# Norm, projections and rotation of the sequence three ahead moved into the tail of a step, and the stored base formed by GpSimd

## What is computed

```
x + attention16(xn) + ffn(xn)
attention16: 16 heads of 8, rotated q and k, distance decay, causal softmax, Wo
ffn: n1 = layernorm(xn); rw = gating(n1)          (8 experts, softmax weights)
     q, k, v = sum over e of rw[e] * (n1 @ proj[e]);  soft = softmax(q k^T) v
     hs = xn + sum over e of rw[e] * (soft @ o_proj[e])
     rw2 = gating(layernorm(hs));  hs + sum over e of rw2[e] * gelu(n2 @ w1[e]) @ w2[e]
```

## Time and profile before

| what | value |
|---|---|
| median of 3 runs | 1389.92 us (1386.5 to 1391.0) |
| the profiled execution | 1386.97 us |
| its span, first to last instruction | 1385.1 us |
| TensorE busy | 1229.1 us, 89% |
| VectorE, ScalarE, GpSimd busy | 73%, 51%, 15% |
| chain that ended last, by engine | PE 68%, DVE 16%, issue 9%, SyncE's queue 4%, DMA 2%, ACT 1% |
| mean granted TensorE clock | 0.966 of 2.4 GHz |

### The profile page before, as it was taken

How to read it: one execution, slowest core, us unless ns; L and a number is a source line. 1 busy time by engine, 2 the same in 40 slices (tenths; PEclk the granted TensorE clock), 3 DMA queues, 4 the chain that set the end, 5 groups by cost and what they waited for, 6 DMA issues and landing times.

```text
span 1385.1 us, 33706 instructions
## 1 busy us (share of the span) xinstructions
PE 1229.1 (89%) x10780; PEld 938.4 (68%) x10780; DVE 1004.5 (73%) x3691; ACT 707.4 (51%) x1281; POOL 211.0 (15%) x325
## 2 busy tenths in 40 slices
PE   1249999999999999999999999999999979999998
PEld 0127777777777677777777777777777766777776
DVE  5547777777777777777777777777777657777653
ACT  1115555555555555555555555555555665555532
POOL 1011111121111222221111111112111200000000
PEclk9659999999999999999999999999999999999999
DMA  5312232222222222222322222222222106544344
GB/s 131 87 63 79 79 90 81 82 82 77 78 78 82 81 80 78 77 77 81 96 97 77 77 79 88 81 82 81 80 80 78 53 26 230 194 154 154 154 169 153
DMA packets 107942, 133.19 MB, mean 96 GB/s; under 512 B 18116, under 2 KB 87252, under 8 KB 99692
## 3 DMA queue, kind: packets, MB, share of 16 engines
q1 hardware_dynamic: 105668, 131.66, 29.6%
q10 hardware_dynamic: 2216, 0.80, 0.2%
HBM read 109.12 MB, written 21.54 MB: 94 GB/s over the span
## 4 chain that ended last, share of the span: by engine, by line
PE 68%; DVE 16%; issue 9%; SPq 4%; DMA 2%; ACT 1%; DVEq 0%; ACTq 0%
PE ps L1448 9%; PE ps L1493 9%; PE ps L1694 8%; PE ps L1449 8%; PE ps L1680 8%; PE ps L1321 4%; PE ps L1458 3%; PE ps L1425 2%; DVE mx L1070 2%; PE ps L1408 2%; SPq L415 2%; PE ps L1371 1%; PE ps L1507 1%; PE ps L1381 1%; DVE xn L894 1%
## 5 line engine op out<-in xcount | busy, mean ns | idle before, releaser
L1070 DVE TENSOR_REDUCE mx<-ps 128x4 f32<-128x1024 f32 (+1 forms) x192 | 234.9, 1223 | 89.4 <-PE ps L1381 80.0
L663 ACT ACTIVATE pr<-ps 128x1024 f32<-128x1024 f32 x192 | 195.8, 1020 | 138.4 <-PE ps L1408 93.7
L558 POOL TENSOR_TENSOR n1s<-rep,n1T 128x256 f32<-128x256 f32 x256 | 176.8, 728 | 254.3 <-DVE mpart L1084 254.3
L669 ACT ACTIVATE ps<-trn 128x1024 f32<-128x1024 bf16 x191 | 197.2, 1032 | 5.1
L1694 PEld LDWEIGHTS ps<-w2s,ats 128*128 128x128 f32 x1024 | 131.7, 192 | 49.8 <-issue 46.8
L1448 PE MATMUL ps<-n1s,wqk 128*128 128x256 f32 x512 | 163.0, 400 | 0.0
L1449 PE MATMUL ps<-n1s,wqk 128*128 128x256 f32 x512 | 152.7, 380 | 0.0
L1458 PE MATMUL ps<-wv,n1s 128*128 128x128 f32 x1024 | 141.6, 281 | 0.0
L1493 PE MATMUL ps<-wop,ats 128*128 128x128 f32 x1024 | 140.0, 294 | 0.0
L842 ACT ACTIVATE n1s<-ps 128x512 f32<-128x512 f32 x128 | 76.5, 597 | 122.6 <-PE ps L1680 121.5
L1694 PE MATMUL ps<-w2s,ats 128*128 128x128 f32 x1024 | 135.7, 276 | 0.5 <-DVE ats L1253 0.5
(11 more groups left out here) (228 smaller groups left out, 2038.3 us busy)
## 6 DMA issues: line engine op xcount, KB each, us to landing
rep<-scr_rw SPq DMA_DIRECT2D x32, 1024.0 KB, 5.0
stk<-scr_rw SPq DMA_DIRECT2D x16, 1024.0 KB, 8.1
stk<-scr_parts SPq DMA_DIRECT2D x896, 16.0 KB
scr_parts<-parts SPq DMA_DIRECT2D x64, 192.0 KB, 2.3
rots<-scr_rw SPq DMA_DIRECT2D x8, 1024.0 KB, 4.8
wqk<-scr_rw SPq DMA_DIRECT2D x8, 1024.0 KB, 8.9
stk<-scr_parts SPq DMA_DIRECT2D x128, 48.0 KB
xt<-in_x SPq DMA_DIRECT2D x32, 128.0 KB, 2.5
```

Source lines behind the costliest of these rows:

```text
L558: pool.tensor_tensor(n1s[:, e], rep[:, par, e], n1T[:, par], ALU.mult).then_inc(n1s_done, 1)
L663: act.activation(pr[:, Q, :, i], ps[:, S2[0]:S2[0] + NF], ACT.Exp).then_inc(exp_done, 1)
L669: act.activation(ps[:, S2[0]:S2[0] + NF], seeds[:, kind:kind + 1].broadcast_to((P, NF, 512)), ACT.Copy).then_inc(seed_done, 1)
L1070: dve.tensor_reduce(mx[:, min(i, 1)].rearrange("p (f h) -> p f h", f=NF)[:, :, h:h + n], ps[:, S1[0]:S1[0] + NF].rearrange("p f (h t) -> p ...
```

## The change

Norm transposes and both projections of sequence n+3 move into the tail of step n, instead of those of n+2 at its start; so does the rotation, between `add_x` and `add_hs`. They use the banks of `S1` and `PVB` there, and the transposed weights and maxima move to `G1`. ScalarE's `evac_norm` is split: `xnT` in the tail, `n1T` and the square at the start of the next step. All six row maxima now lie beside the gating's links, and `soft_max`, `normalise` and `soft_norm` at other links. GpSimd forms base, behind its `scale`. The diff, cut to its core (eight columns of indentation removed):

```diff
-GATE_MAX_AT = (7, 12, 17, 22)
+GATE_MAX_AT = (2, 7, 11, 16, 20, 24)
...
+FIRST, LATER = (G0, G1, G1), (S1[0], S1[1], PVB)
...
+    def add_base(n, u):
+        pool.wait_ge(hs_done, n + 1)
+        pool.wait_ge(xa_done, n + 1)
+        pool.wait_ge(base_stored, 16 * n)
+        hv = hs[:, T * n:T * n + T] if isinstance(n, int) else hs[:, bass.ds(n * T, T)]
+        pool.tensor_tensor(bs[:, u], hv, xa[:, u], ALU.add).then_inc(base_done, 1)
...
         if n_x:
             scale(n + 1, 1 - u)
+        add_base(n, u)
...
-    def evac_norm(b, par):
+    def evac_norm_x(b, banks):
         act.wait_ge(xzT_out, b + 1)
+        act.activation(xnT[:], ps[:, banks[0], 0:S], ACT.Copy).then_inc(xnT_done, 1)
+    def evac_norm_1(b, par, banks):
+        act.wait_ge(xzT_out, b + 1)
         if not isinstance(b, int) or b > 1:
             act.wait_ge(n1s_done, E * (b - 1))
-        act.activation(xnT[:], ps[:, G0, 0:S], ACT.Copy).then_inc(xnT_done, 1)
-        act.activation(n1T[:, par], ps[:, G0, S:2 * S], ACT.Identity, bias=lnp[:, 1:2],
+        act.activation(n1T[:, par], ps[:, banks[0], S:2 * S], ACT.Identity, bias=lnp[:, 1:2],
...
+        if not isinstance(b, int) or b > 1:
+            act.wait_ge(mT_out, b)
         act.wait_ge(rw_stored, 16 * b)
-        act.activation(rwT[0:E * T, 0:P], ps[0:E * T, S1[1], 0:P], ACT.Copy).then_inc(rwT_done, 1)
+        act.activation(rwT[0:E * T, 0:P], ps[0:E * T, G1, 0:P], ACT.Copy).then_inc(rwT_done, 1)
...
-        act.activation(mT[:], ps[0:3 * H, S1[0], 0:S // 2].bitcast(BF16), ACT.Copy).then_inc(mT_done, 1)
+        act.activation(mT[:], ps[0:3 * H, G1, P:P + S // 2].bitcast(BF16), ACT.Copy).then_inc(mT_done, 1)
...
-            evac_norm(n + 2, u)
+            evac_norm_1(n + 2, u, LATER)
         exps(n, 0)
...
         evac_pv(n, 1)
         if n_x >= 2:
+            evac_v(n + 2, u)
+        if n_x == 3:
+            evac_norm_x(n + 3, LATER)
+        if n_x >= 2:
             evac_weights(n + 2)
-            evac_v(n + 2, u)
         if n_x:
             evac_max(n + 1)
...
+    evac_norm_x(2, LATER)
...
-    def rotate(b, beside=None):
-        c = Chain(dve, rot_chain, b, ROT_LINKS, beside)
+    def rotate(b, banks):
+        c = Chain(dve, rot_chain, b, ROT_LINKS)
+        half = "p (a t) -> p a t"
         dve.wait_ge(rot_q_out, b + 1)
-        c.link(dve.tensor_tensor(rott[:, 0], ps[:, G1].rearrange("p (a t) -> p a t", a=2), cs[:, 0], ALU.mult))
+        c.add(dve.tensor_tensor(rott[:, 0], ps[:, banks[1]].rearrange(half, a=2), cs[:, 0], ALU.mult))
+        c.wait()
         c.add(dve.tensor_tensor(rot[:, 0], rott[:, 0, 0], rott[:, 0, 1], ALU.add))
         dve.wait_ge(rot_k_out, b + 1)
-        c.link(dve.tensor_tensor(rott[:, 1], ps[:, G1].rearrange("p (a t) -> p a t", a=2), cs[:, 1], ALU.mult))
+        c.add(dve.tensor_tensor(rott[:, 1], ps[:, banks[2]].rearrange(half, a=2), cs[:, 1], ALU.mult))
+        c.wait()
         c.link(dve.tensor_tensor(rot[:, 1], rott[:, 1, 0], rott[:, 1, 1], ALU.add))
...
         ins.then_inc(hs_done, 1)
-        dve.wait_ge(hs_done, n + 1)
-        dve.wait_ge(xa_done, n + 1)
-        dve.wait_ge(base_stored, 16 * n)
-        dve.tensor_tensor(bs[:, u], hv, xa[:, u], ALU.add).then_inc(base_done, 1)
...
         def beside_gating(k):
             next(norm, None)
             if k in GATE_MAX_AT:
-                next_max(2 + GATE_MAX_AT.index(k))
-            if k == 11:
+                next_max(GATE_MAX_AT.index(k))
+            if k == 17:
+                soft_max(n)
+            if k == 18:
                 normalise(n, 0)
-            if k == 14:
-                soft_max(n)
-            if k == 20:
+            if k == 28:
                 soft_norm(n)
         if n_x >= 2:
-            rotate(n + 2, beside_rotation)
-            next_max(1)
             gating(n + 2, T, 0, gate1, LG1, NORM1, 1, beside_gating)
             run(norm)
...
         add_x(n, u)
+        if n_x == 3:
+            rotate(n + 3, LATER)
         add_hs(n, u)
...
     max_parts(0)
+    rotate(2, LATER)
...
-    def norm_T(b, free):
+    def norm_T(b, banks, free):
...
-                ins = pe.transpose(ps[:, G0, (T * k + i) * P:(T * k + i + 1) * P], src[:, i], ident[:])
+                ins = pe.transpose(ps[:, banks[0], (T * k + i) * P:(T * k + i + 1) * P], src[:, i], ident[:])
...
-    def proj(b, side, prev):
+    def proj(b, side, banks, prev):
...
-            ins = mm(ps[:, G1, k * S:(k + 1) * S], wa[:, 2 * side + k], xnT[:], start=True, stop=True)
+            ins = mm(ps[:, banks[1 + side], k * S:(k + 1) * S], wa[:, 2 * side + k], xnT[:], start=True, stop=True)
         ins.then_inc((rot_q_out, rot_k_out)[side], 1)
...
-    def weights_T(b, old):
+    def weights_T(b, free):
         pe.wait_ge(rw_out, 3 * (b + 1))
-        if old:
-            pe.wait_ge(s1_read, UNITS * b)
-        else:
-            pe.wait_ge(rwT_done, b)
-        pe.transpose(ps[0:E * T, S1[1], 0:P], gt[:, 6, 0:T].rearrange("p i e -> p (i e)"), ident[:]
+        free()
+        pe.transpose(ps[0:E * T, G1, 0:P], gt[:, 6, 0:T].rearrange("p i e -> p (i e)"), ident[:]
                      ).then_inc(rwT_out, 1)
...
-        if k == 0:
-            pe.wait_ge(rwT_done, b + 1 if not isinstance(b, int) or b else 2)
-            pe.wait_ge(mT_done, b)
+        if k == 0 and front is not None:
+            pe.wait_ge(n1T_done, front + 1)
+            pe.wait_ge(rot_chain, ROT_LINKS * front + 1)
...
-        pv = ps[:, S1[0], 0:S // 2].bitcast(BF16)
+        pv = ps[:, G1, P:P + S // 2].bitcast(BF16)
...
+            if front is not None:
+                pe.wait_ge(rot_chain, ROT_LINKS * front + 3)
...
-    def soft_scores(n, free):
+    def soft_scores(n):
         pe.wait_ge(qkT_done, 2 * (n + 1))
-        free()
+        pe.wait_ge(hs_done, n)
...
-                unit1(n + 1, 1 - u, k)
-        if n_x >= 2:
-            norm_T(f, lambda: pe.wait_ge(ats_done, len(ATS_CHUNKS) * n))
+                unit1(n + 1, 1 - u, k, f if n_x >= 2 else None)
         unit2(n, u, 0)
         qk(n, 0)
-        if n_x >= 2:
-            proj(f, 0, lambda: pe.wait_ge(hs_done, n))
         qk(n, 1)
...
         if n_x >= 2:
-            proj(f, 1, lambda: pe.wait_ge(rot_chain, ROT_LINKS * f + 1))
             logits(f)
...
         qk(n, 6)
+        next_max(2)
         qk(n, 7)
-        pv(n, u, 0)
+        pv(n, u, 0, f if n_x >= 2 else None)
         if n_x == 0:
             logits2(0)
-        next_max(2)
+        next_max(3)
         unit2(n, u, 3)
-        soft_scores(n, (lambda: pe.wait_ge(rot_chain, ROT_LINKS * f + 3)) if n_x >= 2 else
-                    (lambda: pe.wait_ge(hs_done, n)))
+        soft_scores(n)
         ve(n, 0)
         out_T(n, 0)
         ve(n, 1)
         ve(n, 2)
-        next_max(3)
+        next_max(4)
         unit2(n, u, 4)
...
-        next_max(4)
+        next_max(5)
         unit2(n, u, 5)
         ve(n, 7)
         if n_x == 0:
             norm_T2(3)
         soft_T(n)
-        next_max(5)
         pv(n, u, 1)
         soft_av(n, (lambda: pe.wait_ge(lg_read, f + 1)) if n_x >= 2 else (lambda: None))
         out_T(n, 1)
         if n_x >= 2:
-            weights_T(f, True)
             proj_v(f, True)
+        if n_x == 3:
+            norm_T(g, LATER, lambda: pe.wait_ge(s1_read, UNITS * f))
+            proj(g, 0, LATER, lambda: None)
+        if n_x >= 2:
+            weights_T(f, lambda: None)
         if n_x:
             max_T(n + 1)
         att_T(n)
+        if n_x >= 2:
+            pe.wait_ge(rwT_done, f + 1)
+        if n_x:
+            pe.wait_ge(mT_done, n + 2)
         oe(n, 0)
         oe(n, 1)
         att_out(n)
+        oe(n, 2)
+        oe(n, 3)
+        if n_x == 3:
+            proj(g, 1, LATER, lambda: pe.wait_ge(xa_done, n + 1))
...
-        for e in range(2, E):
+        for e in range(4, E):
             oe(n, e)
...
     for k in range(UNITS):
         unit1(0, 0, k)
+    norm_T(2, LATER, lambda: pe.wait_ge(s1_read, UNITS))
+    proj(2, 0, LATER, lambda: None)
+    pe.wait_ge(rwT_done, 2)
     max_T(0)
+    proj(2, 1, LATER, lambda: None)
     step(0, 0, 3)
```

More of the change, by code:

```diff
@@ L813, in _ @@
             for b in range(2):
-                evac_norm(b, b)
+                evac_norm_x(b, FIRST)
+                evac_norm_1(b, b, FIRST)
                 evac_logits(b)
@@ L1181, in next_max @@
                         row_max(n + 1, k)
-                def beside_rotation(k):
-                    if k == 1:
-                        next_max(0)
                 norm = (layer_norm(n + 3, 1 - u) if n_x == 3 else layer_norm2(0) if n_x == 1 else
@@ L1206, in step @@
                 else:
-                    for k in range(1, ROT_LINKS + 1):
-                        beside_rotation(k)
-                    next_max(1)
                     if n_x == 0:
@@ L1227, in _ @@
                 norm = layer_norm(b + 1, 1 - b)
-                rotate(b)
+                rotate(b, FIRST)
```

(35 more changed lines are left out.)

## The result

The changed kernel took 1491.78 us (median of 4, 1483.31 to 1492.58) against 1389.76 us: ratio 1.0724, 95% interval 1.0681 to 1.0767. The forecast was 1456 with a range of 1412 to 1475: slower, by the forecast mechanism, but the loss is 102 us where 67 were worked out.

A forecast was written before the change was run, and what follows sets the result against it. TensorE, busy for 89% of the span, was taken to bound the kernel. 28 x (1.75 + 1.2) = 82.6, -14.4 old clock falls, -0.9: +67.3 on 1386.97, 1454.3; half of 2.95 added, 1456, range 1412 to 1475.

The forecast's parts named there:

- the forecast mechanism: Late base delays the `xt` load, gating and `unit1` number 1; TensorE idles 2.9 us and its clock falls; chance 0.60.
- The waits that go: TensorE's tail, `pv` to next step: the waits for weights and `att` go, 1.3 + 0.3 us.
- The load of `xt`: SyncE queue behind base: base at 3.15, `xt` issued at 4.6, landed at 7.1; the old 6.7 us to spare is gone.
- Landing at 7.1: `xt` lands 7.1 us into the step, 2.5 after its issue at 4.6, while gating starts at 4.7.
- The rest of the step: From `unit1` number 1: 8.9 us to `unit2`(4), 4.5 to `pv`(1), 11.3 to the next step.
- The price of the wait: `unit1` number 1 waits from 6.3 to 9.25, 2.9 us idle; the step is 1.75 longer than the steady 32.2.
- the sum without a clock fall: Whole step: 9.25 + 8.9 + 4.5 + 11.3 = 33.95 us.
- rounding the landing down to 7.0: First maximum put at 8.05 to 9.25, its start from 7.0 + 1.05 although the landing was 7.1.
- The clock: TensorE's clock falls behind the 2.9 us idle in nearly each step: 1.2 us taken, bounds nothing and 1.6.
- The rows at 5.13 us: Old kernel's last step: 5.13 us wait ahead of `att_T`, behind which eight `oe` products took 1.92 at the lower clock.
- that the clock would hold: Rival: TensorE stalls once per step but its clock does not fall, +33.7, 1421 to 1424 us; chance 0.20.
- that the load would be in time: Rival: `xt` lands before about 5.3, so `bn_stats` does not wait; by 4.8, 1359 us; chance 0.12.

The follow-up runs named there:

- e1: Changed kernel with SyncE's load of `xt` for the sequence three ahead moved ahead of the wait for base: 1369.97 us, ratio 0.9877.
- e3: Changed kernel with six extra never-read products on TensorE in the wait ahead of `unit1` number 1: 1445.0 us, ratio 1.0405.
- e9: Changed kernel with `add_hs` put back ahead of the rotation in VectorE's tail: 1405.58 us, ratio 1.0105.
- e10: Changed kernel with three extra never-read products on TensorE in the wait ahead of `unit1` number 1: 1461.21 us, ratio 1.052.
- e2: Changed kernel with base formed by VectorE again, right behind `add_hs`, the rotation staying ahead: 1442.96 us, ratio 1.0357.
- e4: Changed kernel with the load of `xt` issued later, behind the weights' spread copy and the store of the parts: 1630.25 us, ratio 1.1741.

## Why the prediction was right, and where it failed

- *The waits that go* (weights, `att`): right, neither is in the list any more.
- *The load of `xt`*: right, and the heart of it. Base at 3.15 was worked out, measured 3.45 (610.32 + 0.72): GpSimd's addition takes 0.72 (0.7 taken), its start 0.28 behind `add_hs` (0.1 taken). Landing at 7.1 was worked out, 7.33 measured in the step shown (607.59 to 614.92) and about 7.55 in the mean.
- *The rest of the step*: `unit2`(4) to `pv` 4.5, measured 4.49 (627.94 to 632.43); tail 11.3, measured 11.25 (632.43 to 643.68); `unit1`(1) to `unit2`(4) 8.9, about 9.1 at the full clock.
- *The price of the wait, first step that failed*: the sum without a clock fall, 33.95, is too small. Measured are 29.24 + 5.49 = 34.7 in the mean; only the quickest steps reach 34. `unit1` number 1 starts some 9.9 into the step and not at 9.25, so it waits 3.3 us and not 2.9: base is 0.3 later, from issue to reading the load takes 2.7 in the mean, where the median landing of 2.5 was put in, and rounding the landing down to 7.0 was wrong by itself. 28 x 0.78 = 22 us.
- *The clock, second step that failed*: the prediction bounded its cost by "nothing, and 1.6 in each step" and took 1.2. Measured: 31.04 less 29.24, 1.8 a step, above its own upper bound. 28 x 0.6 = 17 us. The two together are 39 us, about the whole error of 36. The upper bound came from falls behind a 1.3 us wait and was treated as the price of one fall, whatever came before it. Behind the 3 us wait the clock can be low for over six us, not three, and that costs up to 3.0. The rows at 5.13 us were in hand and should have been read for the length of the slow stretch, which is over six us there too (granted clock 0.80, 0.50, 0.50, 0.50 in the slices of 2 us from 1130, then 0.99).
- *Rivals*: that the clock would hold (0.20), and that the load would be in time (0.12), both fell. The first rested on the Trainium skill, "TensorE: Matmul & The Clock Gate", "Why this matters for your kernels", read strictly as a limit on gaps; the runs disagree with it in that reading, since every wait that averaged 1.7 us and more had its price in the clock, and those of 0.9 (e1) and 0.7 (e3) had none. Its other advice, to keep TensorE busy without a break, is what e3 does, and there the trace agrees: the granted clock was 1.00 from 300 to 900 us.

The clock's cost beside the wait of `unit1` number 1, from the same two rows of each run (us per step; the waits are means from 300 to 900 us, the rest means of 26 steps):

| run | wait | `logits` to `unit1`(1) | from there to `logits` | less 29.24 |
|---|---|---|---|---|
| e3 | 0.7 | 5.34 | 29.24 | 0 |
| e1 | 0.9 | 2.95 | 29.24 | 0 |
| e9 | 1.7 | 3.87 | 29.67 | 0.4 |
| e10 | 2.1 | 5.52 | 29.81 | 0.6 |
| e2 | 2.8 | 4.95 | 30.19 | 0.95 |
| changed kernel | 3.3 | 5.49 | 31.04 | 1.8 |
| e4 | 8.4 | 10.37 | 31.25 | 2.0 |

In e4, 8.1 us of a step are slow, of which 4.3 lie behind the wait; the rest lies in it and costs nothing. Length alone does not decide: in e3 single waits of up to 1.3 us passed without a fall, while in nine of 29 steps of the kernel before a fall followed the wait of 1.3 us. What else decides is not shown.

## What to carry to other kernels

When work is moved ahead of an instruction, list what queues behind that instruction's semaphore on other engines, down to the last load in a queue in order, and compare old and new slack: here 6.7 us of slack on one load became -2.5, and moving that load up in its queue turned 7% slower into 1.2% faster. Price a new wait on TensorE above its own length: here 0.9 us cost nothing more, and waits of 1.7 to 3.3 us cost a quarter to a half more by the clock. Where a load sets the step, put its mean time to landing into the sum and not the median. After prefetching work into a tail, put independent products between a result and its evacuation; that was worth 38 us more.

## What the runs showed of the hardware

- Useless work made the kernel faster: six products of 0.43 us per step, never read, took 47 us off, because the granted clock stayed at 1.00 instead of falling to 0.50 for over six us in half of the steps.
- A 128 KB load took 2.4 us from issue to landing in the changed kernel (median), and 6.1 when it stood behind a 1 MB copy and a store (e4).
- An addition of 128x256 on GpSimd took 0.72 us and started 0.28 us after VectorE's last instruction; on VectorE it took 0.42.
